# Moving three small loads between issue queues at the start of a fused gather, FFN and layer-norm kernel

## The reference

```python
w = weights[conditions]
h = einsum('bct,bcd->bdt', x, w)                   # the "hidden" rows, 4096 x 256
r = top_k(h @ gate_w, 2)[0].sum(-1)                # gate_w 256 x 8
y = square(relu(h @ up_w)) @ down_w + (h @ expert_weight) * r   # up_w 256 x 1024
out = x + layernorm(y) * gamma + beta
```

## Time and profile before

| | us |
|---|---|
| runs | 229.64, 229.46, 229.46 |
| median | 229.46 |
| the profiled execution, device time | 229.29 |
| its span, first to last record | 227.6 |
| PE busy in the span | 220.9 (97%) |
| DVE, POOL, ACT busy | 160.9, 131.4, 106.4 |

### The profile page before, as it was taken

One profiled execution on the slowest core, in us unless ns is written; L12 is line 12 of the kernel. 1 busy time (PEld: TensorE's weight loads), 2 busy tenths in 40 slices (PEclk: granted clock), 3 DMA queues, 4 the chain that ended last, 5 costly groups with the idle time before them and its releaser, 6 DMA issues.

```text
span 227.6 us, 3998 instructions
## 1 busy us (share of the span) xinstructions
PE 220.9 (97%) x1260; PEld 191.4 (84%) x1260; DVE 160.9 (71%) x352; ACT 106.4 (47%) x187; POOL 131.4 (58%) x131
## 2 busy tenths in 40 slices
PE   7899999999999999999999999999999999999992
PEld 2798888888888889888889888888888888888892
DVE  6587965777667777667667766577766766777885
ACT  3379865444555345534545444544454444444000
POOL 3758795665545763656455764366555575557411
PEclk9999999999999999999999999999999999999999
DMA  3877123030603010000200002000020002000031
GB/s 98 231 213 230 50 59 103 10 98 7 187 10 98 9 66 30 0 0 3 92 0 0 3 0 95 3 0 0 0 95 1 0 0 68 28 0 0 10 108 69
DMA packets 17177, 11.81 MB, mean 52 GB/s; under 512 B 6660, under 2 KB 16900, under 8 KB 17156
## 3 DMA queue, kind: packets, MB, share of 16 engines
q1 hardware_dynamic: 15460, 10.43, 15.1%
q10 hardware_dynamic: 1280, 1.07, 1.4%
q0 software_dynamic: 416, 0.05, 0.2%
HBM read 7.35 MB, written 4.19 MB: 51 GB/s over the span
## 4 chain that ended last, share of the span: by engine, by line
PE 94%; DMA 1%; issue 1%; DVE 1%; ACTq 1%; POOLq 0%; POOL 0%; ACT 0%; DVEq 0%
PE up_ps L337 39%; PE down_ps L431 25%; PE down_ps L433 13%; PE hid_ps L303 5%; PE moe_ps L449 3%; PE moe_ps L448 3%; PE moe_ps L447 3%; DMA wd<-in_L_cond_weights_dram 1%; PE down_ps L303 1%; ACTq L513 1%; DMA cond_row<-in_itok_B_dram 1%; POOLq L46 0%; POOL rstd L697 0%; DVE result L615 0%; DVE stats L588 0%
## 5 line engine op out<-in xcount | busy, mean ns | idle before, releaser
L682 POOL TENSOR_TENSOR sq_lo<-square,sq_hi 128x512 fp32r<-128x512 f32 x64 | 84.4, 1322 | 77.0 <-DVE square L553 77.0
L431 PE MATMUL down_ps<-down_hl,sq_hi 128*128 128x512 f32 x248 | 88.8, 393 | 0.0
L553 DVE SCALAR_TENSOR_TENSOR square<-up_ps,relu 128x512 f32<-128x512 f32 x64 | 44.0, 687 | 37.3 <-ACT relu L491 28.2
L433 PE MATMUL down_ps<-down_hl,sq_lo 128*128 128x256 f32 x248 | 69.6, 280 | 0.0
L431 PEld LDWEIGHTS down_ps<-down_hl,sq_hi 128*128 128x128 f32 x248 | 46.5, 188 | 10.8 <-issue 0.3
L491 ACT ACTIVATE relu<-up_ps 128x512 f32<-128x512 f32 x64 | 38.2, 596 | 35.8 <-PE up_ps L337 35.7
L337 PE MATMUL up_ps<-hid_hi,up_hi 128*128 128x512 f32 (+1 forms) x136 | 52.8, 391 | 0.3 <-ACT hid_hi L476 0.3
L337 PE MATMUL up_ps<-hid_hi,up_lo 128*128 128x512 f32 (+1 forms) x136 | 51.1, 379 | 0.0
L433 PEld LDWEIGHTS down_ps<-down_hl,sq_lo 128*128 128x128 f32 x248 | 46.7, 188 | 2.4
L493 ACT ACTIVATE sq_hi<-relu 128x512 fp32r<-128x512 f32 x64 | 40.6, 634 | 2.0
L337 PE MATMUL up_ps<-hid_lo,up_hi 128*128 128x512 f32 (+1 forms) x136 | 40.6, 381 | 0.0
(11 more groups left out here) (62 smaller groups left out, 193.3 us busy)
## 6 DMA issues: line engine op xcount, KB each, us to landing
x_sb<-in_x_dram SPq DMA_DIRECT2D x7, 512.0 KB, 4.2
out_dram<-result SPq DMA_DIRECT2D x7, 512.0 KB, 3.0
wd<-in_L_cond_weights_dram SPq DMA_DIRECT2D x111, 4.0 KB, 1.5
x_sb<-in_L_ffn_down_w_dram SPq DMA_DIRECT2D x2, 512.0 KB, 4.7
x_sb<-in_x_dram ACTq DMA_DIRECT2D x2, 256.0 KB, 2.9
result<-in_L_ffn_up_w_dram ACTq DMA_DIRECT2D x2, 256.0 KB, 2.9
result<-in_L_ffn_up_w_dram SPq DMA_DIRECT2D x1, 512.0 KB, 4.7
out_dram<-result SPq DMA_DIRECT2D x4, 128.0 KB, 1.7
```

What stands on the lines that cost most here:

```text
L431: pe.matmul(dst[:, :], a_hi, down_hl[:, c, :, :].rearrange("p s t -> p (s t)"), start=(c == 0), stop=False)
L433: mm = pe.matmul(dst[:, T:2 * T], a_lo, down_hl[:, c, 0, :], start=False, stop=(c == CH - 1))
L553: dve.scalar_tensor_tensor(square[:, c % 2, :], up_ps[c % UPB][:, :], 0.0, relu[:, c % 2, :], ALU.max, ALU.mult).then_inc(square_done, 1)
L682: pool.tensor_tensor(sq_lo[:, j % 2, c, :], square[:, c % 2, :], sq_hi[:, j % 2, c, :].bitcast(f32), ALU.subtract).then_inc(sq_lo_done, 1)
```

## The change

Three loads change places. SP issues `up_w` part 1 in the place where it issued the other 112 conditions, ahead of its wait for the first 16. ACT no longer issues `up_w` part 1 behind `split_up(0)`; `x` half 1 is the first load there. POOL issues the load of the other 112 conditions as its first instruction, ahead of its memset. No square, wait, product or other instruction is changed; `cond_flat` is only defined further out, so that POOL can use it.

```diff
+        cond_flat = cond.rearrange("(o b) -> o b", o=1)
+
         def load_up(queue, part):
...
-            cond_flat = cond.rearrange("(o b) -> o b", o=1)
             sp.dma_start(cond_row[:, 0:TILES * Q], cond_flat[:, 0:TILES * Q]).then_inc(cond_first_landed, 16)
-            sp.dma_start(cond_row[:, TILES * Q:ROWS_B], cond_flat[:, TILES * Q:ROWS_B]).then_inc(cond_later_landed, 16)
+            load_up(sp, 1)
             sp.wait_ge(cond_first_landed, 16)
...
             split_up(0)
-            load_up(act, 1)
             load_x_first(act, 1)
             hidden_first(0, 0)
...
+            pool.dma_start(cond_row[:, TILES * Q:ROWS_B], cond_flat[:, TILES * Q:ROWS_B]).then_inc(cond_later_landed, 16)
             pool.memset(minus_half[:, :], -0.5).then_inc(consts_ready, 1)
             pool.wait_ge(cond_first_landed, 16)
```

## The result

The changed kernel takes 230.51 us (median of 6 runs, 230.47 to 230.67), the kernel before 229.55 us in the same runs (229.39 to 229.78): a ratio of 1.0041, 95% interval 1.0028 to 1.0054. It is slower by 0.96 us. The prediction said 229.4, at most 229.85. The profiled execution of the changed kernel took 230.51 us with a span of 228.9, so the two traces are 1.22 us apart in device time and 1.3 in span.

The account below looks back on a forecast made before the run. PE's work from 7.74 us on, once batch 7's square had landed, was taken to bound the kernel. +0.02 (issue pace) - 0.05 (gap at 14.4) = -0.03 us on the median 229.46 gave 229.43, rounded to 229.4; range 229.0 to 229.85.

Parts of the forecast that it names:

- part 1: SP issues up's second quarter ahead of its wait: hidden, except +0.02 us for batch 7's square, which misses the longer backlog.
- The term: Slower pace of issue of ACT's squares on full DMA engines sends batch 7 out 0.02 to 0.04 us later; taken +0.02.
- its own sign of being wrong: The forecast is wrong if PE's first product with `up_w` starts before 7.4 or after 8.1 us.
- the other sign: The forecast is wrong if a wait appears on PE behind the first product with `up_w`; no size given.
- the load behind it: ACT's large load issued at 5.05, behind batch 7's square, may lengthen its landing from 1.8 to 2.0 us; nothing taken.
- the cover of group 1: PE waits for group 1 until 6.64 anyway, so group 0 may come 0.6 us later at cost 0.
- Parts 2 and 3: ACT issues `x` half 1 one place earlier, gain 0; POOL issues the other conditions, cost 0.
- part 3: POOL issues the other conditions at about 0.95, covered by 0.5 us; they land by 4; cost 0.
- Part 4: What is late next on PE: the gap at 14.4, of which PE can take 0.07 us; 0.05 taken as gain.
- Rival 2: Slower: squares queue behind up's second quarter in SP's queue, batch 6 takes 2.6 us, PE begins 0.57 later: 230.0; chance 0.09.
- Rival 3: Slower: POOL's first issue holds up DVE's first memset; free to some 0.7 us, 1 us gives 229.7; chance 0.03.
- Rivals 1 and 4: Faster, batch 7's square lands sooner: 229.2, chance 0.18; nothing, no wait of PE moves: 229.46, chance 0.66 together with the forecast.

Follow-up runs that it names:

- e5: Kernel before, with POOL issuing its squares 8 to 12 only when group 0's four squares have landed: 235.53 us against 229.53; batch 7 landed in 1.6 us.
- e8: Changed kernel, with POOL's squares issued only when group 0's squares have landed: 235 to 236 us.
- e4: Changed kernel, with only half of up's second quarter (128 KB) ahead of SP's wait, the rest behind its first four squares: 230.14 us, ratio 1.0021.
- e1: Changed kernel without its POOL part: SP issues the other 112 conditions, then up's second quarter right behind: 230.34 us, ratio 1.0033.
- e6: Changed kernel, with ACT rounding the expert weights (`eg_hi`) ahead of its first relu: 229.87 us, ratio 1.0027.
- e15: Changed kernel, unaltered, run again beside e16 on the same chip: 230.42 us, ratio 1.0049 to the kernel before.
- e16: The kernel of e6 again, run beside e15: 229.80 us, ratio 1.0018 to the kernel before.
- e7: Kernel before, with ACT issuing up's second quarter and `x` half 1 only behind its two roundings of the hidden rows: 235 to 236 us.
- e2: Kernel before with the POOL part alone: POOL issues the other conditions first, SP nothing in their place: 229.60 us, ratio 1.0000.
- e10: Changed kernel, with SP issuing up's second quarter behind its first four squares and ACT rounding the expert weights ahead of its first relu: 229.55 us, ratio 0.9995.
- e12: As e5, with POOL issuing five loads of 16 rows of 8 bytes in its squares' place: batch 7 landed in 1.7 us.
- e13: As e5, with POOL issuing five loads of 16 rows of 256 bytes in its squares' place: batch 7 landed in 1.8 us.
- e14: As e5, with POOL issuing five loads of 32 rows of 8 bytes in its squares' place: batch 7 landed in 1.8 us.
- e3: Changed kernel, with SP issuing up's second quarter behind its squares 0, 2, 4, 6 instead of ahead of its wait: 230.18 us, ratio 1.0020.

## Why the prediction was wrong

**The class and the range.** It forecast no change, 229.0 to 229.85, with 0.12 on slower; it is slower by 0.96 us.

**The step that failed is in part 1: "A square issued then has its data moved at over 5.5 us, and the longer backlog is gone by 4.7. So they don't meet it."** Both halves of the first sentence came true: the backlog ended at about 4.75, and batch 7's last data packet went at 5.87 in both kernels. The step from there to "they don't meet it" failed, because it took the landing for the end of the data. The squares issued from 3.06 on had been held by the backlog and came out of it together; by the traces their counts then landed at the highest rate seen anywhere, and as SP, ACT and POOL add three squares in 0.52 us, the delay of the first was handed on to the last (e5 and e8 show that the squares of the three queues hold each other up). The term was +0.02 and measured +0.90 at the first product: +0.37 with half of the load (e4), +0.60 with the load alone (e1), +0.74 to +0.93 with POOL's part (e6, e15, e16). The first product at 8.64 was past the 8.1 that the prediction had named as its own sign of being wrong, and the wait for `eg_lo` was the other sign. The sign of this was in the trace of before, in rows that the prediction did not show: the squares of the kernel before took longer from one to the next after the DMA engines had gone idle (SP's from 1.5 or 1.6 up to 1.8, ACT's from 1.7 or 1.8 up to 2.0). The prediction suspected the load behind it of ACT's 2.0; e7 shows 2.1 without that load, and e5 1.6 without POOL's squares.

**Part 1, the other terms**: up's first quarter landed at 5.37, later than the 5.0 to 5.2 it was given, but in time (ACT rounded it at 5.39 instead of 5.04, PE never waited for it), and the pace of issue stayed (4.65 against 4.64). Group 0 came at 6.39 instead of 5.40, 0.3 us of it a wait and the rest longer warming products; the cover of group 1 held since that was later still.

**Parts 2 and 3** were right where they stood: `split_up(1)` starts right behind ACT's roundings (8.66, with PE's 8.64), no wait for `x` half 1, and e2 shows POOL's part at nothing by itself. Two readings in part 3 were off at no cost: POOL's issue began at 1.48 and not at 0.95, so that it ended at 2.17, with none of the 0.5 us of cover left (POOL's first square went out at 3.65, before at 3.71), and its load landed at 5.5 and not by 4. What it adds beside the load on SP, 16 counts in place of 1 among the squares', was not seen.

**Part 4 was right in its term and wrong in what is late next.** The gap at 14.4 closed by 0.10 us (0.07 forecast). But DVE, no longer late, then came to `eg_lo` ahead of ACT's `eg_hi` and behind POOL: 1.82 us instead of 0.71. That cost 0.47 us in the trace and 0.62 between e15 and e16, and was no term and no rival. The Trainium skill, SBUF — State Buffer, the section on the shared port pair, has the rule: a VectorE instruction with two inputs in SBUF and a GpSimd instruction that reads SBUF exclude each other, and the one issued second waits for the whole of the first. The trace agrees: `eg_lo` ends 0.57 us behind POOL's instruction, and takes 0.70 when it comes first. The prediction had looked up that section for the memsets alone.

**The rivals.** Rival 2 had the direction and the kind of cause (the new load ahead of the squares), with 0.09. Its place was wrong: SP's batch 6 took 2.4 us and did not decide; ACT's batch 7 did. So was its condition, that data must still be moving at 5.7. Rival 3 did not occur: DVE's two memsets start at 1.09 and 1.63 as before, beside POOL's issue of 0.69 us from 1.48. Rivals 1 and 4 are out.

**Whether the two terms are the whole.** By medians of e15 and e16, 230.42 - 229.80 = 0.62 us is `eg_lo`, and 229.80 - 229.47 = 0.33 is what remains of the late squares. Removing both (e10) leaves 0.9995. How 0.9 at the first product becomes 0.33 at the end is only in part shown: against the profile of before, e16 has +0.93 at the first product, +0.83 at chunk 4 and +0.77 at block 1, and where the rest came back was not found.

## What to carry to other kernels

When a load is moved ahead of many small DMAs, it is not enough that its bytes are gone before those of the last one are due: a landing is data and then counts. Ask whether the small ones come as fast as their counts land. A landing time that grows from one to the next, with the DMA engines nearly idle, says that they do; then every delay at the head reaches the tail. And when an engine is made earlier, look at which instruction of POOL it will now meet: an order that held only because DVE was late is part of the schedule.

## What the runs showed beside this

A PE that stands for long is paid for twice. In e5 PE waited 3.8 us for POOL's squares, of which the last landed 5.1 us after its issue, behind the large loads. The granted clock of e5, before, in and after that wait:

```profile
8.00:10.00 2.00, 1.76 (x13) 1.34 (x11) 0.70 (x2) 0.51 (x1) 1.20 (x3) 1.00 0.81 207
12.00:14.00 2.00, 0.33 (x1) 0.36 (x2) 0.00 (x0) 0.00 (x0) 1.76 (x4) 0.50 0.89 269
16.00:18.00 2.00, 2.00 (x11) 2.00 (x11) 1.80 (x3) 0.14 (x1) 0.00 (x0) 0.50 1.07 330
20.00:24.00 4.00, 4.00 (x29) 3.44 (x28) 2.69 (x3) 3.90 (x8) 2.61 (x3) 1.00 0.40 119
```

The clock fell to the lower level, 1.2 GHz, during the wait and stayed there for over 4 us of full work (a conditioning group of eight products took 2.05 us instead of 1.05), so a wait of 3.8 us made 6 us of device time (235.53 against 229.53). e7, e8, e12, e13 and e14 did the same, which is why only landing times were read from them. In the changed kernel no wait of PE behind its warming was over 1 us, and the column stayed at 1.00.

The ten warming products took 3.87 us in the profiled execution of the kernel before and 4.45 in that of the changed one, at the same clock column of 1.00; 4.45 is also in e3, e4, e6 and e10, and 3.86 in e5. In e10 it set the start of group 0. The products themselves say more than the column: in the kernel before the first seven last 0.63 us (the very first 0.61) and start 0.43 apart, and the last two last 0.38, start to start 0.22; in the changed kernel all ten are of the slow kind. So the engine worked at the lower level at first, which the column does not show, and the moment of its rise differs between executions. What decides that moment was not tried.
